# Issuing two loads of two queues before the engines' programs, and taking one square root before a mask, in a graph layer with layer norm

## What is computed

```python
masks = (relation[None] == rel_ids[:, None, None, None]).astype(x.dtype)
h = einsum('rbnm,bmd->rbnd', masks, x)
y = einsum('rbnd,rdo->bno', h, weight) + bias
out = layernorm(x + y, axis=-1)          # (z - mean) / sqrt(var + 1e-5)
```

## Time and profile before

| | |
|---|---|
| runs | 110.38 us median of 3 (109.97 to 110.46) |
| the profiled execution | 110.12 us |
| its span, first to last instruction | 108.2 us |
| granted TensorE clock | 0.986 of full |
| busy share | PE 92%, PEld 85%, DVE 78%, ACT 79%, POOL 68% |
| DMA | 42.21 MB, mean 390 GB/s over the span |
| chain that ended last, by engine | DMA 57%, PE 24%, ACT 6%, DVE 6%, SPq 3% |

### The profile page before, as it was taken

The page is one execution under the profiler, slowest core; times in us unless marked ns, Lnnn a source line. Parts: engine busy times, 40 slices in busy tenths (PEclk is TensorE's granted clock), DMA queues, the critical chain, the costliest instruction groups (busy, mean ns, idle before and its releaser), DMA issues.

```text
span 108.2 us, 3036 instructions
## 1 busy us (share of the span) xinstructions
PE 99.6 (92%) x1100; PEld 92.3 (85%) x1100; DVE 84.0 (78%) x251; ACT 85.4 (79%) x103; POOL 73.3 (68%) x137
## 2 busy tenths in 40 slices
PE   5979998998999999999999999999999999999800
PEld 5947997998999999989998999899988999999700
DVE  1045879357979999798979997889888998997880
ACT  1346959969969896999699979997899788886850
POOL 3000800096089799989998999989998985923880
PEclk9999999999999999999999999999999999999995
DMA  2999999999999999999999999999999999998145
GB/s 53 359 418 415 421 416 431 436 427 404 431 430 433 407 431 418 430 427 419 428 418 425 428 427 424 424 416 434 427 418 430 424 421 424 413 424 345 47 197 197
DMA packets 7793, 42.21 MB, mean 390 GB/s; under 512 B 865, under 2 KB 994, under 8 KB 4194
## 3 DMA queue, kind: packets, MB, share of 16 engines
q1 hardware_dynamic: 7488, 40.96, 91.3%
q10 hardware_dynamic: 290, 1.05, 2.4%
HBM read 37.81 MB, written 4.19 MB: 388 GB/s over the span
## 4 chain that ended last, share of the span: by engine, by line
DMA 57%; PE 24%; ACT 6%; DVE 6%; SPq 3%; issue 1%; DVEq 0%; ACTq 0%
DMA adj_sb<-adj 57%; PE h_ps L662 11%; ACT bytes_of L525 4%; PE y_ps L674 4%; PE ids_t L640 3%; PE h_ps L714 3%; SPq L385 2%; PE ids_t L631 2%; DVE mask_t L832 1%; ACT mask_t L571 1%; DVE z_lo L817 1%; DVE stats L845 1%; DVE x_sb L895 1%; DVE moments L856 1%; ACT z_hi L563 0%
## 5 line engine op out<-in xcount | busy, mean ns | idle before, releaser
L525 ACT ACTIVATE bytes_of<-adj_sb,offset 128x2048 fp8e4<-128x2048 int32 x32 | 64.1, 2003 | 4.4 <-DMA adj_sb<-adj 3.5
L832 DVE TENSOR_SCALAR mask_t<-ids_t 128x1024 uint16<-128x1024 uint16 x62 | 40.4, 682 | 12.5 <-PE ids_t L631 11.2
L662 PE MATMUL h_ps<-mask_t,x_hi 128*128 128x256 bf16 (+1 forms) x232 | 29.2, 269 | 1.3 <-DVE mask_t L832 0.9
L662 PE MATMUL h_ps<-mask_t,x_lo 128*128 128x256 bf16 (+1 forms) x232 | 29.4, 269 | 0.2 <-DVE x_lo L900 0.2
L452 POOL TENSOR_TENSOR x_sb<-x_sb,bias_sb 128x1024 f32<-128x1024 f32 x8 | 19.0, 2380 | 10.0 <-ACT bias_sb L585 9.5
L491 POOL TENSOR_SCALAR x_sb<-x_sb,rstd,shift 128x128 f32<-128x128 f32 x55 | 23.8, 449 | 0.9
L662 PEld LDWEIGHTS h_ps<-mask_t,x_hi 128*128 128x128 f16 x232 | 21.1, 98 | 3.7 <-DVE mask_t L832 1.3
L662 PEld LDWEIGHTS h_ps<-mask_t,x_lo 128*128 128x128 f16 x232 | 21.9, 98 | 2.8 <-DVE x_lo L900 0.4
L443 POOL TENSOR_TENSOR x_lo<-x_sb,x_hi 128x1024 f16<-128x1024 f32 x6 | 12.9, 2145 | 8.2 <-ACT x_hi L538 7.8
L640 PE MATMUL ids_t<-ident,bytes_of 128*128 128x128 bf16 x192 | 16.2, 227 | 0.0
L640 PEld LDWEIGHTS ids_t<-ident,bytes_of 128*128 128x128 bf16 x192 | 14.7, 148 | 1.3 <-ACT bytes_of L525 1.0
(11 more groups left out here) (85 smaller groups left out, 84.0 us busy)
## 6 DMA issues: line engine op xcount, KB each, us to landing
adj_sb<-adj SPq DMA_DIRECT2D x28, 1024.0 KB, 24.3
adj_sb<-adj SPq DMA_DIRECT2D x8, 512.0 KB, 8.7
out<-x_sb SPq DMA_DIRECT2D x7, 512.0 KB, 21.8
x_sb<-x SPq DMA_DIRECT2D x6, 512.0 KB, 23.4
x_sb<-x ACTq DMA_DIRECT2D x2, 512.0 KB, 6.6
out<-x_sb SPq DMA_DIRECT2D x2, 256.0 KB, 2.1
w_sb<-weight SPq DMA_DIRECT2D x1, 64.0 KB, 5.9
bias_row<-bias ACTq DMA_DIRECT2D x1, 0.5 KB
```

Source lines behind the costliest of these rows:

```text
L525: nc.scalar.activation(bytes_of[:, at % ROOM].rearrange("p n t -> p t n"), adj_sb[:, slot, 2 * k:2 * k + 2, :], ACT.Square, scale=SLOPE, b ...
L662: last = nc.tensor.matmul(h_ps[g.bank][:, to], part[:, g.b % 2, j, :], mask_t[:, g.b % 2, j, cols], start=(j == 0 and part is x_hi), stop= ...
L832: nc.vector.tensor_scalar(mask_t[:, b % 2, :, u * P:(u + 1) * P].bitcast(UINT16), ids_t[bank_of(turn)][:, :, :].bitcast(UINT16), 1 << bit, ...
```

## The change

The first two DMAs of SyncE and of ScalarE are issued by a new function, called before the block that holds the engines' programs. They keep their semaphores, sizes and their order within each queue. In ScalarE's program the square root of the batch `full` is written ahead of the mask of unit 5 instead of behind it.

```diff
+        def first_loads(sp, act):
+
+            act.dma_start(units_of(x_sb[:, 0], 0, 0, J), rows_of(x, 0, 0, J)).then_inc(s_x[0], 16)
+            sp.dma_start(adj_sb[:, 0, 0:1, :], rows_of(adj, 0, 0, 1)).then_inc(s_unit[0][0], 16)
+
+            act.dma_start(units_of(x_sb[:, B - 1], B - 1, 0, J), rows_of(x, B - 1, 0, J)).then_inc(s_x[B - 1], 16)
+            sp.dma_start(w_sb[:, 0, :], weight[0]).then_inc(s_w, 16)
+
+        first_loads(nc.sync, nc.scalar)
         block = ctx.enter_context(nc.Block(no_gpsimd_drain=True))
...
-            load_unit(0, 0)
-            sp.dma_start(w_sb[:, 0, :], weight[0]).then_inc(s_w, 16)
             for u in range(1, J):
                 load_unit(0, u)
...
-            act.dma_start(units_of(x_sb[:, 0], 0, 0, J), rows_of(x, 0, 0, J)).then_inc(s_x[0], 16)
-
-            act.dma_start(units_of(x_sb[:, B - 1], B - 1, 0, J), rows_of(x, B - 1, 0, J)).then_inc(s_x[B - 1], 16)
             act.dma_start(bias_row[:, :], bias.rearrange("(a d) -> a d", a=1)).then_inc(s_bias, 16)
...
             for k in (c.first // 2, e.first // 2):
                 check(a.b, k)
+            root(full)
             mask_second(c.units[1])
-            root(full)
             mask_second(d.first)
             normalise(full, full.units[4:5])
```

## The result

The changed kernel takes 109.82 us (median of 22 runs, 109.50 to 110.18), the one before 110.08 (22 runs, 109.72 to 110.46). The ratio is 0.9973, 95% interval 0.9962 to 0.9985: of 110.08 that is 0.30 us less, between 0.17 and 0.42. (The medians differ by 0.26.) The profiled execution took 109.81 us, its span 108.0 us against 108.2.

The account below looks back on a forecast made before the run. Load issue, then DMA engines bound the start; TensorE, VectorE's small steps and the queued last store bound the end. Span 108.2 - 0.02 - 0.17 = 108.0, 109.93 profiled, 110.2 as median; range 109.7 to 110.65, own range 110.05 to 110.35.

Parts of the forecast that it names:

- Part A: Start of SyncE's and ScalarE's queues: first two loads issued ahead of the branch come earlier; entered as 0.02 us gain.
- so the branch costs at least 0.02 us and at most 0.07 us: Start: branch priced from the 0.07 us barrier-to-load gap and the 0.05 us gap between loads; 0.03 us taken.
- Rival 3: Start: slower, since the moved branch must fetch its target and SyncE's unit loads stall; 111.9 us, chance 0.05.
- Rival 2: Start: first loads don't wait for the barrier and go out nearly half a microsecond sooner; 109.8 us, chance 0.08.
- Part B, the root in the hole: ScalarE near the end: the 0.29 us root of `full` fits a 0.31 us idle gap, mask of unit 5 unmoved.
- GpSimd 0.5 us earlier: Near the end: GpSimd's steps behind the reciprocal shift by 0.5 us, `ra`'s store issued at about 104.55, not 105.05.
- follows the statistics, which end at 98.03: VectorE near the end: with the root done early, the reciprocal starts behind the statistics, 0.51 us earlier than 98.54.
- The tail: Last two stores: `rb`'s issue stays at 105.5 but no longer waits behind `ra`'s data; 0.17 us gain.
- Rival 1: Tail gain doesn't come, as the last store is slow for another cause; 110.35 us, A alone, chance 0.13.
- GpSimd's work under VectorE's: Near the end: GpSimd's normalising moves beside other VectorE instructions; rows showed no lengthening, so nothing entered.

## Why the prediction was right

The prediction was 0.19 us less, the measured difference 0.30 (0.17 to 0.42), and the range holds the time. The level, 110.2, was 0.4 too high: 0.3 of it because the median of three runs, 110.38, lay above that of 22, 110.08. So the forecast's own narrower range, 110.05 to 110.35, does not hold the 109.82.

- **Part A, entered at 0.02 us.** The step "so the branch costs at least 0.02 us and at most 0.07 us" failed. It took the difference of two gaps, 0.07 behind the barrier and 0.05 between loads, for the branch. Taken away, the branch left the first gap at 0.07; put between two loads, it left that gap as it was (the load before ends at 1.19 + 0.43 = 1.62, the next starts at 1.66). It costs nothing that the trace shows, at either place. Rival 3 falls with it: SyncE did not stand still behind the branch. The Trainium skill's rule (Runtime: NRT & Kernel Launch, Instruction fetch mechanics) allows that for a near target; what a far one costs, no run here shows. Rival 2 falls too, as the first DMA waits for the barrier like the branch did.
- **Part B, the root in the hole.** Right: 96.82, and the mask of unit 5 unmoved at 97.21.
- **GpSimd 0.5 us earlier.** 0.6 was measured. The step that the reciprocal "follows the statistics, which end at 98.03" was a little late: it starts at 97.95, before the end shown for them. `ra`'s store came at 104.47, not 104.55.
- **The tail, entered at 0.17 us.** The span and the last landing shrank by 0.2. That the last store waits for the data of the one before is shown by the data in two stretches, by the store taken out altogether, and by all ten traces together: with 0.44 to 0.46 us between the two stores the last one landed after 2.2 us, with 0.54 after 2.1, and with 0.84 or more, or no store ahead of it, after 2.0. Rival 1 is out. (The stretch of data in the earlier trace rows runs to the end of the row, 107.3, so it is 1.4 us and not 1.3; the argument stands.) Two things stay open. `ra`'s store took 2.2 us in the changed kernel with nothing ahead of it, so a landing can be longer for other reasons too. And all these stores went through SyncE's queue; whether one of another queue would wait as well, no run shows.
- **GpSimd's work under VectorE's, entered at nothing.** The sum was right, the reason wrong. The rows I took for "no contention" were of GpSimd's own duration and of statistics. The steps with two inputs from SBUF are held: before, `twice`, `rstd` and `shift` took 0.19, 0.23 and 0.21 us; after, 0.30, 0.16 and 0.16; with GpSimd idle 0.16 each. Over 0.16 each, that is 0.15 us before and 0.14 after. The hold had moved from three steps to one, and it was luck that the sum stayed. Here the Trainium skill's rule (GPSIMD Engine Reference, specification table) was right and my reading of the rows wrong; the trace agrees with it.

That the times show 0.30 and the profile 0.20 needs no further cause: 0.20 lies in the interval, and the root alone gives the same, 0.9969, with loads that did not move.

## What to carry to other kernels

Look at the DMA engines' own view of the tail before at the engines' timelines: two stores that are issued closer together than the data of the first takes make the last one late, and work that is off every engine's critical path (here a square root for another batch) can shorten the program by parting them. Before pricing an instruction without a row as the difference of two gaps, look for a place without it; issuing loads ahead of a program's branch was worth nothing. When GpSimd and VectorE work side by side at the end of a kernel, lay GpSimd's instructions beside VectorE's small steps. And when the last landing has been made earlier, look at what every engine waits for behind it: here a flag that was written 0.6 us later ended the program instead.

## What the runs showed of the hardware

A small VectorE step with two SBUF inputs takes 0.16 us with GpSimd idle and up to 0.30 under a running GpSimd unit of 0.45 us. In the ten traces, all eight steps that started 0.16 to 0.22 us into such a unit ended with it, to 0.01 us. In the changed kernel `twice` runs from 104.15 to 104.45, and GpSimd's second unit ends at 103.55 + 0.89 = 104.44. In the run with the loads alone it was `rstd`:

```profile
104.27 0.48 POOL L498 TENSOR_SCALAR x_sb<-x_sb,rstd,shift 128x128 f32<-128x128 f32 x1
```

```profile
104.27 0.16 DVE L884 SCALAR_TENSOR_TENSOR twice<-once,last_guess 128x4 f32<-128x4 f32 x1
104.46 0.30 DVE L889 SCALAR_TENSOR_TENSOR rstd<-twice,last_guess 128x4 f32<-128x4 f32 x1
```

Both end at 104.75 or 104.76. `twice`, which started together with GpSimd's unit, kept its 0.16, and GpSimd's took 0.48 instead of the usual 0.45. That looks as if the one that comes second waited for the end of the other, but other traces don't bear it out. `twice` before the change also started together with a unit (both at 104.14), took 0.19, and GpSimd's kept its 0.45. And a step that starts only 0.05 us into a unit is not held to its end. With `found` last, `twice` ran from 104.25 to 104.46 under a unit from 104.19 to 104.64; `shift` before the change took 0.21 in the same way, and in the runs with the loads alone and without `ra`'s store it took 0.18. Of the four steps that began in a unit's last 0.04 to 0.07 us three took 0.16, and one, in the run with the root alone, 0.21. So it is shown that either can lengthen the other, and by how much, but not the rule by which one of them gets its turn.
